# Most tiles of a deformable convolution move into the attention loop, with a Newton reciprocal root in their norm

## The reference, cut to what matters

```python
x = x + deformable_conv(group_norm(x), offset_w, offset_b, weight, bias)   # x: 8 x 64 x 32 x 32
t = tokens(x)                                                              # 8 images x 1024 tokens x 64
t = t + attention(layer_norm(t), w_q, w_k, w_v, w_o)                       # 16 heads of 64, causal, rope
t = t + spectral_ffn(layer_norm(t), ...)                                   # four prefixes, gated
# deformable_conv: offsets = conv3x3(x); for each of 9 taps a bilinear sample (4 corners) of x
#                  at the shifted place; out = sampled (576 values a token) @ weight + bias
# layer_norm(t)  = (t - mean) / sqrt(var + 1e-5), over the 64 channels
```

## Time and profile before

| Quantity | Value |
|---|---|
| median of three runs | 4111.8 us |
| profiled execution, own time | 4112.0 us |
| its span, first to last instruction | 4110.2 us |
| mean granted TensorE clock over the span | 0.87 |
| TensorE busy | 3286.9 us, 80% |
| VectorE busy | 2073.0 us, 50% |
| ScalarE busy | 1432.6 us, 35% |
| GpSimd busy | 1538.1 us, 37% |

### The profile page before, as it was taken

How to read it: one execution, slowest core, us unless ns; L and a number is a source line. 1 busy time by engine, 2 the same in 40 slices (tenths; PEclk the granted TensorE clock), 3 DMA queues, 4 the chain that set the end, 5 groups by cost and what they waited for, 6 DMA issues and landing times. The chain is left out here.

```text
span 4110.2 us, 65594 instructions
## 1 busy us (share of the span) xinstructions
PE 3286.9 (80%) x21207; PEld 2369.0 (58%) x21207; DVE 2073.0 (50%) x3068; ACT 1432.6 (35%) x2244; POOL 1538.1 (37%) x1314
## 2 busy tenths in 40 slices
PE   5333333333599999999999999999999939999998
PEld 1122222222366666666666666666666629898988
DVE  2344344344555555555555555555555555565656
ACT  0000000001144444444444444444444425454545
POOL 0577777777233333333333333333333320000000
PEclk8555555555699999999999999999999969999999
DMA  3533333333455555555545455555455533343333
GB/s 85 151 94 92 91 92 92 92 91 94 120 126 121 125 122 123 124 123 124 123 122 126 122 123 124 123 124 123 122 125 122 123 95 116 108 136 109 134 108 108
DMA packets 277334, 472.28 MB, mean 115 GB/s; under 512 B 91529, under 2 KB 103833, under 8 KB 277017
## 3 DMA queue, kind: packets, MB, share of 16 engines
q1 hardware_dynamic: 249624, 395.85, 37.2%
q0 software_dynamic: 27648, 75.53, 6.2%
HBM read 243.92 MB, written 22.29 MB: 65 GB/s over the span
## 5 line engine op out<-in xcount | busy, mean ns | idle before, releaser
L1034 ACT ACTIVATE attention_probs<-attention_pss 128x896 f32<-128x896 f32 (+4 forms) x768 | 621.3, 809 | 1003.7 <-PE attention_pss L901 994.2
L412 POOL DMA_INDIRECT deform_gat<-table,deform_idx x576 | 670.5, 1164 | 208.0 <-issue 164.2
L1083 DVE TENSOR_REDUCE attention_mx<-attention_pss 128x2 f32<-128x1024 f32 (+3 forms) x520 | 520.6, 1023 | 333.0 <-PE attention_pss L923 188.0
L967 PE MATMUL attention_psY<-attention_probs,attention_xt 128*64 128x64 f32 (+7 forms) x4386 | 645.7, 408 | 0.2 <-issue 0.2
L898 PE MATMUL attention_pss<-attention_QA,attention_KA 128*128 128x512 f32 (+4 forms) x1536 | 542.0, 407 | 15.9 <-ACT attention_probs L1034 12.0
L1121 POOL TENSOR_TENSOR attention_qk<-attention_tA,attention_tB 128x512 f32<-128x512 f32 x260 | 333.8, 1284 | 543.3 <-DVE attention_tB L1098 527.7
L1541 DVE SCALAR_TENSOR_TENSOR spectral_eo<-spectral_psE,spectral_sig,spectral_eo 64x512 fp32r<-64x512 f32 x512 | 383.9, 750 | 263.8 <-ACT spectral_eo L1520 259.2
L1444 PE MATMUL spectral_psE<-spectral_tz,spectral_up 128*128 128x256 f32 (+2 forms) x3072 | 507.5, 324 | 4.6 <-DVE spectral_eo L1541 4.6
L1444 PEld LDWEIGHTS spectral_psE<-spectral_tz,spectral_up 128*128 128x128 f32 x3072 | 470.6, 188 | 45.1 <-DVE spectral_eo L1541 6.3
L480 PE MATMUL deform_psT<-kept_ident,deform_smp 128*128 128x128 f32 (+1 forms) x320 | 85.0, 431 | 479.8 <-DVE deform_smp L439 479.8
L1097 DVE TENSOR_TENSOR attention_tA<-attention_pss,attention_cosT 128x512 f32<-128x512 f32 x260 | 179.2, 689 | 552.4 <-PE attention_pss L937 463.8
(11 more groups left out here) (164 smaller groups left out, 3747.4 us busy)
## 6 DMA issues: line engine op xcount, KB each, us to landing
attention_QA<-attention_nat_h SPq DMA_DIRECT2D x520, 128.0 KB, 2.3
spectral_tz<-phis SPq DMA_DIRECT2D x128, 320.5 KB, 4.6
spectral_tz<-phis SPq DMA_DIRECT2D x128, 320.0 KB, 4.2
attention_xb<-xn SPq DMA_DIRECT2D x67, 512.0 KB, 3.5
attention_wt<-wsplit SPq DMA_DIRECT2D x67, 512.0 KB, 4.2
attention_KA<-attention_nat_h SPq DMA_DIRECT2D x260, 128.0 KB, 2.3
attention_KB<-attention_nat_h SPq DMA_DIRECT2D x260, 128.0 KB, 2.3
attention_KA<-attention_nat_l SPq DMA_DIRECT2D x260, 128.0 KB, 2.3
```

Of the source, the lines that this page charges most:

```text
L412: pool.indirect_dma_start(gat[:, r, k, :, :].rearrange("p q c -> p (q c)"), None, d.table.rearrange("r q c -> r (q c)"), bass.IndirectOffs ...
L967: ins = pe.matmul(psY[C * half:C * half + C, c0:c1], xt[:, kt_, :], probs[:, q + c0:q + c1], start=first, stop=(j == NS - 1), skip_group_c ...
L1034: act.activation(probs[:, pstep[j]:pstep[j] + width], pss[:, slot, lead:lead + width], ACT.Exp, scale=float(E) ** -0.5).then_inc(s_act, 1)
L1083: ins = dve.tensor_reduce(mx_far[:, :, i - 4] if k0 else mx[:, :, i], scores, AX.X, ALU.max)
```

## The change

Only the first ten tiles (`FIRST`) are made in the deform stage, in five iterations written out, two neighbouring tiles of one image in each. The other 54, and ten tiles of filler after them (their weights and row numbers are zero), are made inside the attention loop, one in each half. The order of tiles is now image by image. The layer norm of a tile made in attention has no square root on ScalarE: VectorE starts from a bit pattern and refines it in four Newton steps.

The order of score steps, units, PV products, GpSimd work and key splits is new as well. Three units are added to each half: `dT` (transposes of the samples), `dR` (the convolution's product and the residual) and `dX` (transpose of the normalised tile). VectorE gets its work at the places of `DEFORM_AT`: three multiplications of 768 elements a partition (`m0` to `m2`), two additions (`a`) and the norm (`s`).

```diff
-                with sp.Fori(0, G) as g:
-                    with sp.Fori(0, NT) as t:
+                for it in range(FIRST // 2):            # FIRST = 10, same on every engine
...
-STEPS = [(0,), (7, 6), (3,), (1,), (4, 5), (2,)]
+STEPS = [(0,), (7, 6), (4, 5), (2,), (3,), (1,)]
...
-    0: [[("rope", 0)],
-        [("rope", 1), ("out",)],
-        [("rope", 2), ("rope", 3)],
+    0: [[("rope", 0), ("rope", 1)],
+        [("rope", 2)],
         [],
-        [("max", "b"), ("max", "d")],
-        [("max", "c"), ("max", "e")]],
-    1: [[("max", "k"), ("max", "a")],
-        [("max", "g"), ("max", "j")],
-        [("max", "f")],
-        [("max", "i")],
-        [("max", "h"), ("out",), ("row",)],
+        [("max", "b"), ("out",), ("rope", 3), ("max", "a")],
+        [("dT",), ("max", "c"), ("max", "d")],
+        [("max", "f"), ("dR",), ("max", "h")]],
+    1: [[("max", "i")],
+        [("max", "e"), ("max", "k")],
+        [("max", "j")],
+        [("max", "g"), ("out",), ("row",)],
+        [("dX",)],
         []],
...
+DEFORM_AT = {(0, 0): ["m0", "m1"], (0, 1): ["m2"], (0, 2): ["a"], (1, 0): ["s"]}
+POOL_ORDER = [("add", 0), ("add", 1), ("lower", 0), ("add", 2), ("lower", 1), ("gather", 0), ("add", 3), ("lower", 2), ("lower", 3), ("token", 0), ("gather", 1), ("token", 1), ("gather", 2)]
+UPPER_AT = {1: [0, 1], 3: [2], 5: [3]}
+NEWTON = 4
-PV_AT = {(0, "before"): -2, (0, "end"): -1, (1, "end"): 0, (3, "before"): 1, (4, "end"): 2, (5, "before"): 3}
+PV_AT = {(0, "end"): -2, (1, "after"): -1, (3, "before"): 0, (4, "before"): 1, (4, "after"): 2, (5, "before"): 3}
...
+                def deform(op, it, k):
+                    step = Chain(dve, s_def, DEF_STEPS * 2 * it + (DEF_STEPS * (k + 1)))
+                    if op[0] == "m":
+                        x = int(op[1])
+                        dve.wait_ge(s_gath[x], 96 * it + (48 * k + 48))
...
+                        dve.tensor_tensor(v, v, w.unsqueeze(2).to_broadcast([P, 12, C]), ALU.mult).then_inc(s_def, 1)
+                    elif op == "a":
...
+                        step(dve.tensor_tensor(v[:, :, 0:2 * C], v[:, :, 0:2 * C], v[:, :, 2 * C:4 * C], ALU.add))
+                        dve.tensor_tensor(smp[:, :].rearrange("p (k c) -> p k c", k=K2), v[:, :, 0:C], v[:, :, C:2 * C],
+                                          ALU.add).then_inc(s_def, 1)
+                    else:
...
+                        step(dve.bn_stats(stats[:, :], tile))
+                        step(dve.bn_aggr(mv[:, :], stats[:, :]))
+                        step(dve.tensor_scalar(var[:, :], mv[:, 1:2], LN_EPS, None, ALU.add))
+                        step(dve.tensor_scalar(rstd[:, :].bitcast(I32), var[:, :].bitcast(I32), -0.5, ROOT_SEED,
+                                               ALU.mult, ALU.add))
+                        for _ in range(NEWTON):
+                            step(dve.scalar_tensor_tensor(out=fix[:, :], in0=rstd[:, :], scalar=-0.5, in1=rstd[:, :],
+                                                          op0=ALU.mult, op1=ALU.mult))
+                            step(dve.tensor_scalar(fix[:, :], fix[:, :], var[:, 0:1], 1.5, ALU.mult, ALU.add))
+                            step(dve.tensor_tensor(rstd[:, :], rstd[:, :], fix[:, :], ALU.mult))
+                        step(dve.tensor_scalar(xn[:, :], tile, mv[:, 0:1], rstd[:, 0:1], ALU.subtract, ALU.mult))
+                        dve.tensor_copy(xt_new[:, k, 1:C], xn[:, 1:C]).then_inc(s_def, 1)
...
+                def gather(x, tile, drawn, done):
+                    if x == 0:
+                        if done is not None:
+                            wait_apart(pool, s_def, done, s_apart)
+                        pool.tensor_copy(idx[:, :], m.IDX[:, tile, :]).then_inc(s_idx, 1)
+                    for n in range(3 * x, 3 * x + 3):
+                        pool.indirect_dma_start(...).then_inc(s_gath[x], 16)
```

More of the change, by code:

```diff
@@ L471, in _ @@
                 pe.wait_ge(s_w, 48)
-                with pe.Fori(0, G * NT) as it:
+                pe.wait_ge(s_xs, 32)
+                for it in range(FIRST // 2):
                     for r in range(2):
@@ L739, in attention_stage @@
         s_row = sem("row")
+        s_gath = [sem(f"gath{x}") for x in range(3)]
+        s_idx = sem("idx")
+        s_def = sem("def")
+        s_xs = sem("xs")
+        s_store = sem("store")
         s_dup = sem("dup")
```

221 lines of the change are left out of this document (161 added, 60 removed).

## The result

The changed kernel takes 3931.17 us (median of four runs, 3920.97 to 3934.62), the kernel before 4111.76: a ratio of 0.9555, 95% interval 0.9537 to 0.9573. It is 4.5% faster; the forecast was 3654 and a range up to 3780, so the gain is well under half of what I foresaw.

What follows compares the result with a forecast made beforehand. It took the deform stage as bound by GpSimd issuing indirect DMAs, attention by TensorE. From 4112.0 us: - 746 (deform loop) + 64 x 4.4 (282, attention's halves) + 6 (once) = 3654 us; 8-in-10 range 3530 to 3780.

Steps and rivals of the forecast that it cites:

- TensorE's units and what they displace: Attention: dR, dT and dX add 2.5 us of TensorE work to each half, bounds 2.2 and 5.0.
- row's DMA, less the loop's head: First score step of a half: a shorter wait for the negated maxima's DMA takes off 0.4 us, bounds 0 and 1.0.
- the norm: Attention: VectorE's 4.0 us norm before reading e makes TensorE stand 1.7 us a half ahead of j, bounds 0 and 4.0.
- the samples' arithmetic: Attention: VectorE's multiplications and sums meeting GpSimd's rope additions cost 0.6 us a half, bounds 0 and 2.7.
- clock of the two stops together: Attention: the sum held nothing for low clock, which stood only as a rival with chance 0.03.
- The deform loop: Deform stage: 32 iterations become five, saving 27 x 27.63 = 746 us; start-up of attention costs 6.
- a rival of its own (3, chance 0.03): Attention: TensorE's pauses lower its clock to 1.2 GHz; slower than before if a half exceeds 46.0 us; chance 0.03.
- two of my own signs: Attention: clock below 0.97 would speak for the clock rival; TensorE waiting elsewhere over 1 us a half would show error.
- the meeting with GpSimd: Attention: VectorE multiplications against GpSimd rope additions, taken at 0.6 us a half; 1.3 by the skill page's lock rule.
- Rivals 1 and 2: Attention: VectorE's work is hidden, half some 36.4 us, 3500 us; or more collisions, 3795 to 3860 us; chance 0.22 each.
- rival 2: Attention: late gathers, full lock or longer norm make a half 41 to 42 us, 3795 to 3860 us; chance 0.22.

Runs made afterwards that it cites:

- e8: Changed kernel without the norm's four Newton steps and with VectorE's multiplications and sums of the samples cut to 64 columns: 3603 us.
- e7: Changed kernel with VectorE's multiplications and sums of the samples cut to 64 columns: 3744 us.
- e6: Changed kernel without the norm's four Newton steps: 3749 us.
- e4: Changed kernel with eight Newton steps in the norm rather than four: 4270 us.
- e15: Kernel before the change, with 20 small dependent VectorE instructions added in every half: 4384 us.
- e10: Changed kernel with all samples' arithmetic between the last score steps of the half before, gathers behind GpSimd's rotation work, norm in two, row unit later: 3739 us.
- e2: Changed kernel with the first two multiplications of the next tile moved to the end of the half before: 3895 us.
- e11: Changed kernel with GpSimd's rotation additions and subtractions cut from 512 to 64 columns: 3771 us.
- the best order: e10 with TensorE's exact wait at the loop's head and the row unit in its old place: 3717 us, on another chip 3813.

## Why the prediction was wrong, by its steps

The steps of a half, as predicted and as measured. The pieces come from the differences between e8, e7, e6 and the changed kernel, and they add up to the whole.

| term, us a half | predicted | measured | from |
|---|---|---|---|
| TensorE's units and what they displace | + 2.5 | + 3.1 | e8's short half 37.07 - 33.98 |
| row's DMA, less the loop's head | - 0.4 | + 0.5 | e8 37.94 - 34.39 - 3.1 |
| the norm | + 1.7 | + 2.1 | e7 - e8: 1.55 stop, 0.6 clock |
| the samples' arithmetic | + 0.6 | + 2.2 | e6 - e8: 1.5 stop, 0.7 clock |
| clock of the two stops together | 0 | + 0.8 | rest |
| sum | + 4.4 | + 8.7 | |

**Right.** The deform loop: - 756 against - 740 with the start-up of attention, since five iterations ran at under 27.63 us each. The norm as a block: 4.1 us from BN_STATS to the copy against 4.0, its stop ahead of `j` 1.55 against 1.7. The wait for the row's DMA at a half's first score step went, and TensorE's three units took 2.3 us against 2.5.

**The failed step: the clock.** I treated low clock as a rival of its own (3, chance 0.03) which should only matter if all was lost, and took 0 in the sum. It doesn't need a slower kernel. In the mean it is 0.6 to 0.7 us for one stop of 1.5 us a half (e6, e7), 2.2 for two, 5.1 with stops of 4.1 us (e4), 2.2 for one of 2.2 us in a kernel otherwise without (e15), none where TensorE stood only 1.4 us every second half (e8). The length of a stop doesn't decide it alone: e10's stops of about 1.5 us brought none in 51 of 53 halves, and e2, with 4.2 us of stops in more pieces, had 0.9. The busy share doesn't either: TensorE was busy 90% in e2 and 94% in e15 (1400 to 2000 us), at clocks of 0.98 and 0.94. What decides stays open. I had argued "against" from a mean of 95% busy; the mean hides what comes right behind a stop. Clock is 2.1 of the 4.3 us by which I missed, and two of my own signs came: a granted clock under 0.97 (0.95), and a wait of over 1 us a half elsewhere (ahead of `a`).

**The second: the meeting with GpSimd.** I took 0.6, near a row in which VectorE lost nothing against an indirect DMA. The Trainium skill's page "SBUF — State Buffer" (Who interferes with whom) speaks of an exclusive lock, for VectorE instructions with two inputs in SBUF against GpSimd's reads. The trace agrees: 1.13 us for one value, ending with the addition; 0.21 for the one-input instruction beside it; the sums and the rotation additions both longer in the changed kernel, as if waiting in turn, and the sums back at their own length in e10 and e11. With that rule I had worked out 1.3; measured are 1.5 of stop, before clock. I should have taken it: the row was of another pair of operations. (That attention had no VectorE instruction with two on-chip inputs outside PSUM was wrong too: the merge in the earlier trace rows is one, of 128x8, and it kept its 0.17 us.) The collision could be seen in the code too, since the additions wait for exactly the readings that stand around the multiplications.

**The third: the head of the loop's body.** The new order puts a score step last in the body, and at the head TensorE waits for all readings, its exponential included: 1.45 us every second half. I had not looked at what the unit before the head would be. I had also counted the row's gain as a gain for every half, while the kernel before had its stop (0.38) only every second one.

**The fourth: a size.** 3.1 for 2.5: the units' own 2.3, and 0.8 which I had left out. No run takes these 0.8 apart: they may be later starts of the neighbouring matmuls or another effect of the new order.

The range failed with the sum. Rivals 1 and 2 had 0.44 together, but the range ended at 3780, so it held nothing of rival 2, which began at 3795; and rival 2 was bounded by collisions alone. Its 422 to 486 us fall short of 558.6, and clock was left out of both ends. Outside the loop 20 us more lie behind the last merge, 13 of them in the spectral stage, which is unchanged; e8, without stops ahead of `a` and `j`, has them too. Half of the 13 are low clock in the trace (11.8 us lost in that stage against 5.2); the cause was not looked for.

## What to carry to other kernels

A stop of TensorE must be priced with what the clock may take behind it. Here that was between nothing (e10, 1.5 us) and about the stop's length again (e15, 2.2 us, and what e4 added); for the changed kernel's own stops it was a bit over half. A mean over a loop can hide two kinds of iterations: look at the first and the last ones apart. Before adding arithmetic with two on-chip inputs to VectorE, look up in the order which GpSimd arithmetic its neighbours release; move it beside indirect DMAs or into a gap. Compare variants a few tens of us apart on one chip: the same program gave 3717 and 3813 us, while the kernel before, run beside it, stayed within 4 us.

## What the runs showed of the hardware that I had not expected

- The low clock came at 0.50 for over 3 us right behind a stop, and a stop of 2.2 us a half in a kernel 99% busy before was enough (e15, 0.94 over 600 us). Stops of about 1.5 us brought it in some halves and not in others: in 40 of the changed kernel's 64, and in 2 of 53 in e10.
- A VectorE instruction of one value took 1.13 us beside a GpSimd addition of 1.27 us, and GpSimd's own went to 2.40 us behind VectorE's long ones.
- Gathers of one address slow other DMAs: on one chip the medians with and without them stand 51 us apart, all of it in the last ten halves. In the changed kernel's own order the same gathers cost nothing: its last ten halves take 43.0 us, as the others do.
- On three of the chips TensorE's results came 1.5 us and more after the end that the records give, in kernels with the gathers inside attention only (not in the kernel before, nor in e15); on one of those the best order took 95 us more.
